# Projections of the first chunk of queries at four other steps, and its first Q and K stacks loaded at other steps

## What is computed

```python
xn = _layernorm(x, axis=-1)
x = x + _L0_attn_ref(xn, Wq, Wk, Wv, Wo) + _L0_ffn_ref(xn, W_gate, b_gate, W1, b1, W2, b2)
xn = _layernorm(x, axis=-1)
x = x + _L1_attn_ref(xn, Wq, Wk, Wv, Wo, bo) + _L1_ffn_ref(xn, We, be, Wg, bg)

# attention, both layers: causal softmax of q k^T / 4, times v, then the output projection
# ffn, layer 0: scores = xn @ W_gate + b_gate, the two best; relu(xn @ W1 + b1) @ W2 + b2, weighted
# ffn, layer 1: softmax gates, the two best rescaled to sum 1; xn @ We + be, weighted
```

## Time and profile before

| | us |
|---|---|
| timed runs: median of 3 (lowest to highest) | 3225.12 (3223.69 to 3232.07) |
| the profiled execution | 3192.34 |
| its span, first to last instruction | 3190.6 |
| PE busy (share of the span) | 3012.9 (94%) |
| DVE busy | 2359.8 (74%) |
| ACT busy | 1980.9 (62%) |
| POOL busy | 1025.1 (32%) |
| granted TensorE clock, mean | 0.982 of 2.4 GHz |

### The profile page before, as it was taken

How to read it: one execution, slowest core, us unless ns; L and a number is a source line. 1 busy time by engine, 2 the same in 40 slices (tenths; PEclk the granted TensorE clock), 3 DMA queues, 4 the chain that set the end, 5 groups by cost and what they waited for, 6 DMA issues and landing times.

```text
span 3190.6 us, 61821 instructions
## 1 busy us (share of the span) xinstructions
PE 3012.9 (94%) x19056; PEld 1580.5 (50%) x19056; DVE 2359.8 (74%) x7245; ACT 1980.9 (62%) x4954; POOL 1025.1 (32%) x1244
## 2 busy tenths in 40 slices
PE   5899999999999999999999999999999999999998
PEld 3454544445455554544445455454545555445443
DVE  5676778777777776878777687777878767677784
ACT  2466666666666666656666666666666666566665
POOL 4115134241522414334151341513324142241512
PEclk8899999999999999999999999999999999999999
DMA  6767455364655635446364554635547364453642
GB/s 188 209 164 215 126 163 156 111 192 118 187 169 153 185 118 171 134 128 182 104 209 142 163 175 124 189 106 159 169 130 212 120 196 148 146 159 99 183 137 77
DMA packets 328101, 496.01 MB, mean 155 GB/s; under 512 B 56832, under 2 KB 242656, under 8 KB 327776
## 3 DMA queue, kind: packets, MB, share of 16 engines
q1 hardware_dynamic: 293536, 416.99, 44.4%
q0 software_dynamic: 24576, 67.14, 6.8%
q10 hardware_dynamic: 9664, 7.93, 0.9%
HBM read 344.19 MB, written 152.84 MB: 156 GB/s over the span
## 4 chain that ended last, share of the span: by engine, by line
PE 80%; DVE 9%; issue 4%; ACT 3%; DMA 1%; SPq 1%; POOL 0%; DVEq 0%; ACTq 0%; another core or an unknown queue 0%; POOLq 0%
PE po L1137 16%; PE pmx L1087 15%; PE pst L1074 14%; PE pst L1121 10%; PE pmx L1207 6%; PE pst L1106 5%; PE pmx L1176 4%; PE pst L1218 4%; PE pst L1095 3%; DVE pmx L836 3%; PE pst L1143 2%; PE pmx L1155 2%; ACT probs L679 1%; DMA xg<-x_slots 1%; DVE x L968 1%
## 5 line engine op out<-in xcount | busy, mean ns | idle before, releaser
L679 ACT ACTIVATE probs<-pst 128x512 f32<-128x512 f32 (+3 forms) x3072 | 1404.6, 496 | 461.6 <-PE pst L1074 431.6
L590 POOL TENSOR_SCALAR_AFFINE_SELECT probs<-probs 128x512 f32<-128x512 f32 x512 | 327.0, 639 | 1800.9 <-ACT probs L679 1798.9
L832 DVE TENSOR_REDUCE rmax<-pmx 128x1 f32<-128x512 f32 x1024 | 668.8, 683 | 140.1 <-PE pmx L1087 131.8
L1074 PE MATMUL pst<-qs,k_first 98*128 98x512 bf16 (+3 forms) x2048 | 692.2, 343 | 34.3 <-issue 18.2
L836 DVE CUSTOM_DVE_ANT_0 pmx<-pmx,mask,rmax 128x128 f32<-128x128 f32 (+3 forms) x1024 | 538.6, 555 | 239.7 <-PE pmx L1087 201.3
L1087 PE MATMUL pmx<-k_first,qs 96*128 96x512 bf16 (+2 forms) x2048 | 669.2, 344 | 21.0 <-DVE rmax L836 6.3
L1137 PE MATMUL po<-probs,v 128*32 128x512 f32 (+3 forms) x6144 | 662.4, 503 | 4.0 <-POOL probs L590 4.0
L836 DVE CUSTOM_DVE_ANT_0 pmx<-pmx,mask 128x128 f32<-128x128 f32 (+3 forms) x1024 | 483.1, 510 | 171.1 <-PE pmx L1087 145.6
L1087 PEld LDWEIGHTS pmx<-k_first,qs 96*128 96x128 bf16 x2048 | 199.2, 98 | 363.9 <-issue 157.7
L1087 PE MATMUL pmx<-k_second,qs 96*128 96x128 bf16 (+3 forms) x1024 | 306.4, 304 | 27.9 <-DVE otok L948 14.1
L1074 PE MATMUL pst<-qs,k_second 98*128 98x512 bf16 (+3 forms) x1024 | 303.7, 303 | 16.4 <-ACT probs L679 9.5
(11 more groups left out here) (121 smaller groups left out, 3349.4 us busy)
## 6 DMA issues: line engine op xcount, KB each, us to landing
wt<-w_tiles SPq DMA_DIRECT2D x161, 513.0 KB
qk_parts<-parts SPq DMA_DIRECT2D x256, 192.0 KB
xg<-x_slots SPq DMA_DIRECT2D x368, 128.0 KB
y_slots<-ys SPq DMA_DIRECT2D x368, 128.0 KB
wt<-w_tiles SPq DMA_DIRECT2D x184, 256.0 KB
qs<-qk_parts SPq DMA_DIRECT2D x128, 192.0 KB
qs<-qk_parts SPq DMA_DIRECT2D x128, 128.0 KB
k_first<-qk_parts SPq DMA_DIRECT2D x64, 192.0 KB, 3.0
```

The costliest lines, as they stand in the source:

```text
L590: pool.affine_select(out=tri, in_=tri, compare_op=ALU.is_ge, fill=0.0, base=0, pattern=[[0, GH], [1, P]], channel_multiplier=-1).then_inc( ...
L679: act.activation(probs[:, u % 2, j, 0:w], ps[:, 0:w], ACT.Exp, scale=DH ** -0.5).then_inc(st_read, 1)
L832: dve.tensor_reduce(rmax0[:, col:col + 1], src, AX_X, ALU.max).then_inc(mx_read, 1)
L1074: pe.matmul(ps[:, 0:w], keys[0:SROWS, j, k % HT * P:(k % HT + 1) * P], qs[0:SROWS, set_no(q, n) % QRING, j, a:a + w], start=True, stop=Tru ...
```

## The change

Four entries of `PROJ` change, all of the first chunk: the projections of column tile 0 go from steps -26 and -24 to -33 and -31, those of tile 1 from -18 and -16 to -24 and -18. The two stores of parts follow them, from -22 and -14 to -29 and -16. Of the stacks of sets 0 to 3, Q moves from -19, -15, -11, -7 to -26, -23, -14, -7, and K from -17, -13, -9, -3 to -27, -20, -12, -4. The scatter stays at -18 to -11 and the first token load at -9. Nothing is added or removed.

```diff
-PROJ = {(0, 0): -26, (0, 1): -24, (0, 2): -18, (0, 3): -16, (1, 0): -10, (1, 1): -8, (1, 2): -2, (1, 3): 0}
-LOAD_Q = (-19, -15, -11, -7, 1, 5, 13, 19)
-LOAD_K = (-17, -13, -9, -3, -1, 9, 16, 25)
+PROJ = {(0, 0): -33, (0, 1): -31, (0, 2): -24, (0, 3): -18, (1, 0): -10, (1, 1): -8, (1, 2): -2, (1, 3): 0}
+LOAD_Q = (-26, -23, -14, -7, 1, 5, 13, 19)
+LOAD_K = (-27, -20, -12, -4, -1, 9, 16, 25)
```

## The result

| | median of the runs, us | lowest to highest | profiled execution, us |
|---|---|---|---|
| before (4 runs, with those ahead) | 3228.6 | 3223.7 to 3233.0 | 3192.3 |
| after (4 runs) | 3297.4 | 3295.2 to 3305.0 | 3295.5 |

The account below looks back on a forecast made before the run. PE, busy 94% of the span, was taken as the bound, so only its idle or lower-clock time could be won. Terms 2.4 + 0 + 20.9 + 0 = 23.3 us off 3225.1 gave 3201.8 us, range 3170 to 3230.

Parts of the forecast that it names:

- Part 3: DMAs at places 30 to 37: with no K stack right behind the store, 20.9 us of PE's stop would go.
- 21% and 64% shares: Stack's shares of the stall at places 35 and 36: 21% of layer 0's 26 us, 64% of layer 1's 24.
- Part 1: Start-up, which nothing covers: 1.0 us off the scatters, 1.4 off the first weights; 2.4 us won.
- Part 2: Projections in steady runs leave places 22 and 32 for 15 and 17, 3.6 us moving along; net 0.
- about 140: Sign at places 35 and 36: their sum over sixteen runs falls to some 140 us instead of 168.
- all of it goes: Rival at places 35 and 36: thinner traffic ends the whole 50 us stop; 3173 us, chance 0.16.
- moves with the store: Rival: all 50 us of stop stay, at places 32 to 34 instead of 35 and 36; 3223 us, chance 0.23.
- two stops for one: Slower rival: PE stops at the store's place 32 and again at places 35 to 37; 3253 us, chance 0.13.
- The rule on SBUF's two sides: PE's stop: transfers cannot slow compute, so thinning traffic gives back nothing of the 50 us; same time as 3223.
- Part 4: SP's order: K stacks one step behind the unit they wait for may delay stores or token loads; cost 0.
- The 32.8 us: Gap from the profiled execution to the timed median of 3225.1 us, unexplained and carried along into the forecast.

Follow-up runs that it names:

- run 5: Not a follow-up: number 5 of the 16 runs (0 to 15) in one execution, each one batch row through one layer in 48 steps.
- the store ahead: Kernel after with projections (0,2) and (0,3) moved to places 22 and 25, second store at place 27, scatter row left long: 3258.4 us, 1.0086 of before.
- Before with waits: Kernel before with GpSimd waiting, at each step with scatters, for the unit's four exponentials before its two scatters: 3157.1 us, 0.9774 of before.
- kernels with short rows: Kernel after, projections (0,2), (0,3) at places 22 and 25, GpSimd waiting for four exponentials before each step's scatters; on two chips 3131.0 and 3128.9 us.
- after, waits: Kernel after with GpSimd waiting, at each step with scatters and a unit, for that unit's four exponentials: 3183.1 us, 0.9845 of before.
- run 11: Not a follow-up: number 11 of the 16 runs (0 to 15) in one execution, one batch row through layer 1 in 48 steps.

## Why the prediction was wrong, point by point

**Part 3 failed, and at its first step**, the cause. From the earlier trace rows I read that "the scatter alone, or with one stack, does not stop PE; the scatter with store, weights, tokens and stack on top of each other does". The row of scatters was not counted as a thing of its own. The earlier trace rows end where the row of six had issued only its first ones, so they could not clear the scatter. The 21% and 64% shares of Part 3 priced a stack that the run with the loads alone shows to be worth nothing (1.0009 of before): the 20.9 us of the sum were for no cause of the stop.

**The missing term** is the low part. In Part 1 I counted it between two scatters as 1.0 us lost; in Part 2 the projection's GpSimd work stood as 1.17 us wherever it goes. That it waits for ScalarE there, and thereby holds the scatters behind it, was in the trace: four scatters, a pause, six. Taking it away gave a row of ten, worth +152.7 us at place 34; one wait put back in its place gave 0.9987 of before.

**Places 35 and 36** went from 168 us (sixteen) to 115, where I had put about 140 (168.4 less my own 20.9 would have been 147.5): the whole old stop went, as in the rival "all of it goes". It had been the tail of the row of six, and the row of ten ends at place 34.

**Places 32 to 34** were named as the place to look for the rival "moves with the store", and that is where the loss is (20.5 us in run 5 against 12.5 in the earlier trace rows). That rival kept the old size, 3223; the size followed the row, and no case of mine reached 3297. The slower rival, two stops for one at 3253, was another mechanism: there is one stop.

**The rule on SBUF's two sides** (the Trainium skill, "SBUF — State Buffer", section "SBUF: two separate sides") says that a transfer cannot slow a compute instruction. I had worked out from it that the cause would not be traffic and that thinning the traffic would give nothing back. The runs agree with that for PE: no idle time at a share of 0.87, 8 us at 0.43. I weighed it too lightly, as one more road to 3223; that time was wrong too, since the other cause grew with the change.

**Part 1 held.** First token load, first weights and first expert product after:

```profile
63.12 0.34 SPq L478 DMA_DIRECT2D xg<-x_slots  x1
...
64.57 0.93 SPq L412 DMA_DIRECT2D wt<-in_w  x2
...
68.32 2.07 PE L1106 MATMUL pst<-xgT,wt 128*128 128x128 f32 x8 [1.16 <-DMA wt<-in_b]
```

64.57 against the 64.8 and 68.32 against the 69 that I named (the earlier trace rows before: 67.27 and 71.26); the first attention product ends at 98.2 instead of 100.7, 2.5 us against 2.4.

**Part 2 held.** Places 22 and 32 together fell by 3.3 us a run, 15 and 17 together rose by 3.1, where I had put 3.6 for both. **Part 4 held:** the projections alone do what the whole change does. But that I counted nothing at places 24 to 26, since a projection stands at place 24 before and after, hid a gain that the forecast had no term for. Place 24 has VectorE waiting for PE, places 25 and 26 PE waiting for VectorE. With the projection at 25, PE works where it had stood idle. Places 24 to 26, run 5, before and with the store ahead:

```profile
1177.50:1193.20 15.70, 13.86 (x86) 6.31 (x78) 12.70 (x40) 10.15 (x24) 2.92 (x3) 0.92 0.58 177
```

```profile
1203.20:1215.50 12.30, 12.30 (x86) 6.48 (x78) 10.61 (x36) 9.23 (x23) 1.82 (x3) 1.00 0.67 189
```

Over all seams this is 2.1 us each (14.4 to 12.3).

**The 32.8 us** between the profiled execution and the median of before, for which no view had shown a reason, seem to belong in part to the same stops. Before with waits stands 74 us under the median of before on its chip, more than the 50 in the profile. The granted clock points the same way: 0.982 in the profiled execution of 3192.3 us, 0.973 to 0.978 in the thirteen of 3224.8 to 3238.3 us on the first chip of the table. The kernels with short rows took nearly the same on two chips (3131.0 and 3128.9), the kernel before 3199 to 3231 on five; that these differences too lie in the stops is argued, not shown.

## What to carry to other kernels

Look at a queue's instructions in the order in which they are issued, and ask of each one that moves what it had kept apart: a waiting subtraction between two scatters was worth 2.3% of this kernel by standing there. When several engines stop together and start together at the end of a row of one engine's instructions, vary the row (its length, its pauses) before pricing the traffic. And put movable work not where its engine has room on average, but where that engine waits for another one.

## What the runs showed of the hardware

- Indirect DMAs that GpSimd issues one behind the other (1.27 us each, three quarters of which the profile shows as busy) hold up the engines behind PE from about the fifth on, for some 1.36 us a piece (PE idle 2.4 us a seam with four and six, 5.4 with eight, 8.1 with ten); with a quarter of the bytes, or of the tokens (1.18 us each), it is the same. Plain DMAs from the same queue don't, nor do indirect ones in pairs with 1.4 us between. Rows of four at most, set apart by the waits (after, waits), still left 0.8 to 2.8 us.
- The gathers of places 42 to 49 are indirect DMAs too, four in a row at places 42 and 43. Before has next to no idle time at place 43 (0.02 us a seam), after has 0.60, up to 1.61 in run 11, with the same four gathers; why, no run shows. Place 43 of run 11, after and before:

```profile
2490.60:2496.30 5.70, 4.09 (x27) 1.69 (x24) 2.47 (x10) 2.88 (x7) 1.75 (x2) 1.00 0.90 292
2412.10:2415.90 3.80, 3.80 (x26) 1.75 (x24) 2.34 (x10) 2.71 (x7) 1.72 (x2) 1.00 0.92 291
```

- By which way a scatter holds PE back stays open. What the trace shows is that the semaphore steps of PE's finished products come late, by 2.1 to 8.9 us in the stop of run 5 above. It is no wait for instructions: in 8 of after's 15 seams none of the instruction queues' transfers runs in the stop or in the 1.5 us ahead of it.
